# The causal mask of every first-pass unit moves from TensorE products into VectorE's row-maximum instructions

## The reference

```python
q = split_heads(x @ Wq + bq)
k = split_heads(x @ Wk + bk)
v = split_heads(x @ Wv + bv)
att = jnp.einsum('bhtd,bhsd->bhts', q, k) * (1.0 / math.sqrt(Dh))
causal = jnp.tril(jnp.ones((T, T), dtype=bool))
att = jnp.where(causal[None, None], att, -jnp.inf)
att = jax.nn.softmax(att, axis=-1)
o = jnp.einsum('bhts,bhsd->bhtd', att, v)
```

## Time and profile before

| | |
|---|---|
| median of 3 runs | 521.52 us |
| lowest and highest of them | 516.39 and 522.48 us |
| span of the profiled execution | 517.1 us |
| TensorE products busy | 468.1 us (91%), 3122 instructions |
| VectorE busy | 374.1 us (72%), 1046 instructions |
| ACT busy | 272.8 us (53%) |
| POOL busy | 252.8 us (49%) |

### The profile page before, as it was taken

The page is one execution under the profiler, slowest core; times in us unless marked ns, Lnnn a source line. Parts: engine busy times, 40 slices in busy tenths (PEclk is TensorE's granted clock), DMA queues, the critical chain, the costliest instruction groups (busy, mean ns, idle before and its releaser), DMA issues. The chain is left out here.

```text
span 517.1 us, 9099 instructions
## 1 busy us (share of the span) xinstructions
PE 468.1 (91%) x3122; PEld 239.6 (46%) x3122; DVE 374.1 (72%) x1046; ACT 272.8 (53%) x571; POOL 252.8 (49%) x344
## 2 busy tenths in 40 slices
PE   3478889999999999999999999999999998899897
PEld 2224334544644553545454453545454454344554
DVE  4687746997589748985699648985789757875165
ACT  2214554775558535765568435764567534755321
POOL 7534356533865077535764077525763251523530
PEclk9857996999999999999999999999999999999999
DMA  4674452332333234323443134323433222003000
GB/s 106 164 171 115 117 152 50 85 94 85 106 99 87 56 113 117 100 69 106 114 101 90 42 111 112 97 61 104 129 83 98 83 77 60 2 2 104 1 21 22
DMA packets 40942, 45.31 MB, mean 88 GB/s; under 512 B 9448, under 2 KB 32520, under 8 KB 40896
## 3 DMA queue, kind: packets, MB, share of 16 engines
q1 hardware_dynamic: 35652, 40.92, 29.9%
q10 hardware_dynamic: 5244, 3.82, 2.6%
HBM read 33.70 MB, written 10.61 MB: 86 GB/s over the span
## 5 line engine op out<-in xcount | busy, mean ns | idle before, releaser
L799 ACT ACTIVATE probs<-s_bank 128x512 f32<-128x512 f32 x320 | 179.9, 596 | 97.2 <-PE s_bank L1199 95.6
L979 DVE CUSTOM_DVE_ANT_0 s_bank<-s_bank,causal_row 128x512 f32<-128x512 f32 (+1 forms) x256 | 156.2, 642 | 28.9 <-PE s_bank L1179 27.3
L1179 PE MATMUL s_bank<-k_stack,q_stack 72*128 72x256 bf16 (+3 forms) x512 | 129.6, 314 | 10.7 <-DVE row_max L979 5.1
L1199 PE MATMUL s_bank<-q_stack,k_stack 75*128 75x128 bf16 (+3 forms) x512 | 120.4, 308 | 15.3 <-DMA q_stack<-max_rows 7.6
L662 POOL TENSOR_SCALAR_AFFINE_SELECT probs<-probs 128x512 f32<-128x512 f32 (+1 forms) x96 | 75.5, 794 | 116.2 <-ACT probs L799 116.0
L1199 PEld LDWEIGHTS s_bank<-q_stack,k_stack 75*128 75x128 bf16 x512 | 43.1, 100 | 92.0 <-ACT probs L799 41.1
L1218 PE MATMUL pv_bank<-probs,v_aug 128*32 128x512 f32 (+3 forms) x1024 | 83.2, 444 | 0.0
L1179 PEld LDWEIGHTS s_bank<-k_stack,q_stack 72*128 72x128 bf16 x512 | 47.3, 100 | 75.0 <-DVE row_max L979 38.5
L984 DVE TENSOR_REDUCE row_max<-s_bank 128x2 f32<-128x512 f32 (+1 forms) x96 | 64.5, 687 | 16.9 <-PE s_bank L1183 16.0
L1218 PEld LDWEIGHTS pv_bank<-probs,v_aug 128*32 128x32 f32 x1024 | 26.1, 110 | 43.8 <-issue 34.2
L1067 DVE SCALAR_TENSOR_TENSOR silu_sb<-tanh_sb,gate_bank 128x512 f32<-128x512 f32 x38 | 26.1, 687 | 21.6 <-ACT tanh_sb L852 21.3
(11 more groups left out here) (183 smaller groups left out, 546.0 us busy)
## 6 DMA issues: line engine op xcount, KB each, us to landing
k_stack<-k_scr SPq DMA_DIRECT2D x96, 96.0 KB
q_stack<-q_scr SPq DMA_DIRECT2D x93, 96.0 KB
coef_all<-coef_scr SPq DMA_DIRECT2D x28, 256.0 KB, 3.9
k_scr<-k_parts SPq DMA_DIRECT2D x32, 96.0 KB, 1.9
q_scr<-q_parts SPq DMA_DIRECT2D x31, 96.0 KB, 1.9
k_scr<-k_parts SPq DMA_DIRECT2D x32, 64.0 KB, 1.8
x_res<-in_L_attn_x SPq DMA_DIRECT2D x8, 256.0 KB, 3.7
x_in<-in_L_attn_x ACTq DMA_DIRECT2D x7, 256.0 KB, 2.8
```

The lines of the kernel that those rows point to most:

```text
L799: nc.scalar.activation(dst, src, ACT.Exp, scale=SCALE).then_inc(exp_done, 1)
L979: nc.vector.tensor_tensor_reduce(out=s1_bank[u % 2][:, 0:w], in0=s1_bank[u % 2][:, 0:w], in1=causal_row[:, T - w:T], scale=1.0, scalar=MAS ...
L1179: final = nc.tensor.matmul(dst[:, w * i:w * (i + 1)], q_stack[0:KROWS, h, P * qt:P * (qt + 1)], k_stack[0:KROWS, h, 0:w], start=(i == 0), ...
L1199: final = nc.tensor.matmul(dst[:, at:at + w], k_stack[0:MROWS, hh, P * j:P * (j + 1)], q_stack[0:MROWS, hh, P * j:T], start=True, stop=True)
```

## The change

VectorE takes the maximum of every unit with the masked instruction, once for each head of the unit; the reduction is gone. TensorE's mask products are gone, and so are `causal` and its two instructions of set-up on POOL. Units 8 and 9 become two masked maxima of 256 elements each, unit 10 four of 128 elements each, every one with its reading of the accumulator; only the last of a unit raises `s1_reduced`. The rest of the diff rewrites the way in which the program walks through the table `ORDER` (a list of turns instead of loops, and a count of the uses of a bank made from that list). The words of the table are the same, and apart from the instructions named no engine's sequence changes.

```diff
-            causal = sb("causal", [P, P], BF16)
...
-            nc.gpsimd.memset(causal[:, :], 0.0).then_inc(const_step, 1)
+            nc.gpsimd.memset(ones_wide[:, :], 1.0).then_inc(const_step, 1)
...
-            final = nc.gpsimd.affine_select(out=causal[:, :], in_=causal[:, :], compare_op=ALU.is_ge, fill=MASKED,
-                                           base=0, pattern=[[-1, P]], channel_multiplier=1)
...
-                    if masked_by_max(a):
-                        if u == 0 and it == 0:
-                            dve.wait_ge(row_masked, 1)
-                        nc.vector.tensor_tensor_reduce(
-                            out=s1_bank[u % 2][:, 0:w], in0=s1_bank[u % 2][:, 0:w], in1=causal_row[:, T - w:T], scale=1.0,
+                    if u == 0 and it == 0:
+                        dve.wait_ge(row_masked, 1)
+                    for i in range(nh):
+                        scores = s1_bank[u % 2][:, w * i:w * (i + 1)]
+                        final = nc.vector.tensor_tensor_reduce(
+                            out=scores, in0=scores, in1=causal_row[:, T - w:T], scale=1.0,
                             scalar=MASKED, op0=ALU.add, op1=ALU.max,
-                            accum_out=row_max[s % 2][:, 0, h, qt].unsqueeze(1)).then_inc(s1_reduced, 1)
-                    else:
-                        nc.vector.reduce_max(row_max[s % 2][:, 0, h:h + nh, qt],
-                                             s1_bank[u % 2][:, 0:nh * w].rearrange("p (h k) -> p h k", h=nh),
-                                             AX_X).then_inc(s1_reduced, 1)
+                            accum_out=row_max[s % 2][:, 0, h + i, qt].unsqueeze(1))
+                    final.then_inc(s1_reduced, 1)
...
-                                                 k_stack[0:KROWS, h, 0:w], start=(i == 0), stop=masked_by_max(a))
-                    if not masked_by_max(a):
-                        diagonal = dst[:, 0:nh * w].rearrange("p (h k) -> p h k", h=nh)[:, :, w - P:w]
-                        final = nc.tensor.matmul(diagonal, ident_bf[:, :], causal[:, :].unsqueeze(1).to_broadcast([P, nh, P]),
-                                                 start=False, stop=True)
+                                                 k_stack[0:KROWS, h, 0:w], start=(i == 0), stop=(i == nh - 1))
```

More of the change, by code:

```diff
@@ L80 @@
 ORDER = {
+    "head": {
+        "pe": "cond xt k q v gates",
+        "dve": "xs cond xn cols k q gates",
+        "act": "xt k q stack v gates",
+        "pool": "xs late",
+        "sp": "stack",
+    },
     "first": {
@@ L168, in task, with turn_task @@
     return (int(parts[1]), parts[0], int(parts[2]) if len(parts) > 2 else 0)
[L171 to L182, removed]
+def turn_task(it, word):
+    if word[0] == "-":
+        return (it - 1, *task(word[1:]))
+    if word[0] == "+":
+        return (it + 1, *task(word[1:]))
+    return (it, *task(word))
+TURNS = [("head", -1), ("first", 0), *(("middle", b) for b in range(1, B - 1)), ("final", B - 1), ("tail", B)]
+ENGINES = ("pe", "dve", "act", "pool", "sp")
+PROGRAM = {e: [turn_task(it, word) for plan, it in TURNS for word in ORDER[plan][e].split()] for e in ENGINES}
 FILL_TAIL = {("y", 0): 2, ("x2t", 0): 9, ("g", 0): 2}
 MISC_TASKS = ("o", "ot", "x2t", "lg", "ct", "xt", "q", "k", "v", "max")
[L190 to L196, removed]
+MISC_RANK = {x: n for n, x in enumerate(
+    x for x in PROGRAM["pe"] if x[2] in MISC_TASKS and (x[0], x[2]) not in ((-1, "k"), (-1, "v")))}
 def misc_at(it, use):
[L201 to L209, removed]
+    return MISC_RANK[(it, *use)]
 def wait_v(eng, b, misc_read, v_read):
@@ L216, in wait_v, with walk @@
     else:
-        eng.wait_ge(misc_read, misc_at(b - 1, (s_of(b - 1, "v"), "v", 0)) + 1)
-def turn_of(s, name, a):
-    return (B - 1, s, name[1:], a) if name[0] == "-" else (B, s, name, a)
+        eng.wait_ge(misc_read, misc_at(b - 1, (0, "v", 0)) + 1)
 def need(eng, sem, value):
-    if not isinstance(value, int) or value > 0:
+    if value > 0:
         eng.wait_ge(sem, value)
[L231 to L243, removed]
+def walk(engine, run):
+    for x in PROGRAM[engine]:
+        run(*x)
 def block_kernel(nc, x, Wq, bq, Wk, bk, Wv, bv, Wo, bo, gamma, beta, router, w_gate, w_up, w_down,
@@ L408, in first @@
         def first(it):
-            return isinstance(it, int) and it == -1
+            return it == -1
         def last(it):
[L412 to L417, removed]
+            return it == B
         def gate_of(it, a):
@@ L533, in run @@
                 if name == "cw":
-                    sp.wait_ge(misc_read, misc_at(it, (s_of(it, "ct"), "ct", 0)) + 1)
+                    sp.wait_ge(misc_read, misc_at(it, (0, "ct", 0)) + 1)
                     for landed in coef_landed:
@@ L555, in has_next @@
             def has_next(it):
-                return not isinstance(it, int) or it < B - 1
-            walk(sp, "sp", run)
+                return it < B - 1
+            walk("sp", run)
             sp.wait_ge(stored, 16 * (B + 1))
@@ L703, in run @@
                     nc.gpsimd.tensor_tensor(cp[2], coef_rest[:, :, :], cp[1], ALU.subtract).then_inc(coef_split, 1)
-            walk(pool, "pool", run)
+            walk("pool", run)
         @block.scalar
@@ L852, in run @@
                     nc.scalar.activation(tanh_sb[:, :], gate_of(it, a)[:, :], ACT.Tanh, scale=0.5).then_inc(tanh_ready, 1)
-            walk(act, "act", run)
+            walk("act", run)
         @block.vector
@@ L1090, in run @@
                                                 (x_in if last(it) else x2)[:, tiles, :], ALU.add).then_inc(out_half if last(it) else gate_read, 1)
-            walk(dve, "dve", run)
+            walk("dve", run)
         @block.tensor
@@ L1141, in run @@
                     nc.tensor.matmul(gate_bank[:, 0:C], bv_rep[:, :], wo[:, :], start=True, stop=True).then_inc(bias_mm, 1)
-                if name == "v" and isinstance(it, int) and it == 0:
+                if name == "v" and it == 0:
                     pe.wait_ge(ffn_in, 16 * FFN_DMAS)
@@ L1286, in run @@
                     if a == 0:
-                        pe.wait_ge(misc_read, misc_at(it, (s_of(it, "x2t"), "x2t", 0)) + 1)
+                        pe.wait_ge(misc_read, misc_at(it, (0, "x2t", 0)) + 1)
                     if a == 0 and it == 1:
@@ L1314, in run @@
                     if a == 0:
[L1315 removed]
+                        pe.wait_ge(misc_read, misc_at(it, (0, "ct", 0)) + 1)
                         pe.wait_ge(x2_ready, it)
@@ L1341, in run @@
                         last_mm.then_inc(down_written, 1)
-            walk(pe, "pe", run)
+            walk("pe", run)
 _INS = ["L0_attn_x", "L0_attn_Wq", "L0_attn_bq", "L0_attn_Wk", "L0_attn_bk", "L0_attn_Wv", "L0_attn_bv",
```

8 lines of the change are left out of this document (3 added, 5 removed).

## The result

The changed kernel takes 548.81 us as the median of 4 runs (544.2 to 549.62), the kernel before 519.7 us (516.39 to 522.48) beside it: a ratio of 1.0549, with a 95% interval of 1.0469 to 1.0629. (A ratio leaves out the runs that took over 1.5% more than the fastest of their kernel; in experiments e1 and e4 those are the ones with the lowest granted clock, so there it understates the loss that the median shows.) The prediction was 526.8, in a range of 516 to 540; the time lies above it. The profiled execution has a span of 547.9 us, 30.8 more than before.

A forecast was written before the change was run, and what follows sets the result against it. No single bound: TensorE and VectorE wait for each other in turn. Six middle batches at +0.89 us give +5.3, first and last 0; 521.5 + 5.3 = 526.8 us, range 516 to 540.

The forecast's parts named there:

- The step from the two pair lengths that the trace showed to the two that it didn't: VectorE's maximum-and-reading pairs: a straight line from 512 and 384 elements gave 0.38 us for 256, 0.25 for 128.
- The sum at a steady clock: Delays at the ends of the four groups of a middle batch: 0.60 + 0.06 + 0.23 = 0.89 us.
- Group 2: Its end: later bank release moves TensorE's waiting product by 0.76 us, partly absorbed before the maxima's transposition; +0.60 us.
- Groups 0 and 1: Their ends: removed mask time turns into waiting; 0 for group 0, +0.06 us for group 1.
- Group 3: Its end: unit 10's four pairs release later, so POOL's split and the maxima's transposition come late; +0.23 us.
- the last rival: TensorE's granted clock falls once more per middle batch, 1.62 us each, giving 536.5 us; chance 0.14.
- TensorE as the bound: Rival: the mask products' 14.1 us come off whole, giving 507.4 us; chance 0.05.
- VectorE as the bound: Rival: all 22 us of VectorE's added time appear, giving 543.5 us; chance 0.09.
- A floor in the pair: Rival: no VectorE pair takes under 0.51 us, losing 38 us in all, giving 559.5 us; chance 0.05.
- The period of 61.6 us: Middle batch: about 57.9 us was forecast; near 60 or more would show that VectorE's time was on the path.
- the granted clock below 1.00: Sign against the forecast: TensorE's granted clock below 1.00 in most middle stretches.
- VectorE's busy time: Sign for the forecast: it rises by some 50 to 65 us, more than 22 because the rows overlap.

The follow-up runs named there:

- e1: Changed kernel with units 8 to 10 of group 2 back to mask product and reduction in every batch; 527.11 us, ratio 1.0067.
- e4: Kernel before without its 96 mask products, reductions kept and nothing put in their place; 533.49 us, ratio 1.0179.
- e7: Kernel before with the second layer norm's statistics moved behind unit 10 of group 2 on VectorE; 545.82 us, ratio 1.0542.
- e2: Kernel before with only units 8 to 10 of group 2 masked by VectorE as in the change; 547.34 us, ratio 1.0546.
- e5: Changed kernel with five products that nothing reads in TensorE's two waits at the end of group 2, each middle batch; 528.53 us, ratio 1.0225.
- e3: Changed kernel with a product of zeros on TensorE where each mask product stood; 552.74 us, ratio 1.0616.

## Why the prediction was wrong

**What held.** The step from the two pair lengths that the trace showed to the two that it didn't (0.38 and 0.25 us) was right to 0.01. The Trainium skill, "VectorE: DVE Perf Modes", section on the TRN2 errata, would give 0.39 and 0.26 as an estimate; the trace lies 0.01 below each. The sum at a steady clock was nearly right too: +0.66 us measured for a middle batch, +0.89 forecast. By its terms:

- *Group 2*, +0.60 forecast: +0.67. Counted from unit 8, TensorE's product that waits for the bank comes 0.69 us later than before, less than the 0.76 of the sum, and nothing absorbs any of it on the way to the transposition of the maxima, where 0.16 had been allowed for. The two errors cancel.
- *Groups 0 and 1*, +0.06: the table's first four lines give -0.01 - 0.22 + 0.15 + 0.04 = -0.04.
- *Group 3*, +0.23: -0.22 + 0.25 = +0.03. The masked unit takes 1.09 us to its release (193.97 to 195.06), 1.14 forecast; and before, the transposition came 0.71 us after POOL's split had begun (180.76, 181.47), now 0.56 (195.15, 195.71): TensorE's own work had held it up by 0.15.

**What failed** is the step that left TensorE's clock out of the sum: the forecast has no term for it, and the last rival, which has one, was wrong in both of its numbers, price and chance. The price, 1.62 us for a fall, was read from one fall of 3.4 us in the kernel before (284 to 287). The trace of before had another, at 75.4 to 85.6 us, three times as long: there group 0, up to the start of group 1, took 14.70 us, and the same stretch of e7 and e2, whose clock stays up there, takes 10.99 and 11.08, so that this fall cost 3.6 to 3.7. The falls of the changed kernel are of that kind and cost 3.97. Six of them are 24 us, the lateness 6 x 0.66 = 4. The other 3 are about 4 in the first batch, where the prediction had 0 with 1 us either way and where the clock is low from 19 to 56 us and again from 63 to 66 (before: 21 to 38 and 41 to 48), and 1 in the second, less the 1.6 of the fall at 284 that the kernel before had. The rival as written, with the other price, would have said 521.5 + 5.3 + 24 = 551.

Its chance was 0.14 because "the longest wait, at 167.92, is moved and not lengthened". That was the wrong wait to look at. The fall comes before that wait, after two shorter ones at the first products of group 3, 0.27 us and none before, 0.61 and 0.31 after. The prediction had worked out the 0.76 us by which these come later, and used it for the path alone. It never asked what TensorE does in that time, although the 0.44 us of removed products, in the same place, make the idle time longer still: it went from 0.44 to 1.27 us. That is the step that failed. The delay was nearly right; that it costs only itself was not. It cost 0.66 us a batch on the path and 3.97 by the clock; e5 shows that without the idle time the same delay is followed by no fall there, and e4 that falls come without any delay.

**The other rivals.** TensorE as the bound: at a steady clock the products were worth 0.77 us a batch, less than half of their own time, so the case against it was right; with the clock as it came, taking them out alone cost time (e4). VectorE as the bound at 543.5 us came near the time by accident: e2 has a quarter of its added instructions and all of the loss. A floor in the pair isn't there.

**The signs that were named.** The period of 61.6 us stood in the list as a sign of VectorE's time, and the granted clock below 1.00 as a sign of its own. Both came; only the second was the cause. A period that is too long must be read with the clock's row beside it. VectorE's busy time rose by 20 us and not by 50 to 65, because the page's line for the engine counts overlapping instructions once; added up over the page's groups (239.3 + 73.2 us after, 156.2 + 64.5 + 36.2 before) it rose by 55.6.

## What to carry to other kernels

Where TensorE runs at its upper level with little idle time to spare, cost a change by what it does to TensorE's *standing still*, place by place, and price a fall by the longest one that the trace shows. Here 0.7 us of added waiting cost 0.7 us on the path and 4 us by the clock, and taking products away without any delay cost more time than it saved. Products that nothing reads, put into waits that are there anyway, gave 6.4 us back to the kernel before and 20 to the changed one.

## What was not expected of the hardware

VectorE's four normalising instructions took 1.11 to 1.12 us in a middle batch of the changed kernel and of the kernel before, 0.28 each, and 2.56 us in the two kernels with the statistics moved, 0.64 each. In the rows of e7 above, POOL's three `AFFINE_SELECT` instructions ran through nearly all of it (292.06 to 294.35). In the last batch they take 2.66 us in the kernel before too, and there too POOL is busy for most of it (447.61 to 449.75, of 447.67 to 450.33). The Trainium skill, "SBUF — State Buffer", section "Who interferes with whom", tells that such an instruction of VectorE can take a pair of ports that it shares with GpSimd, and that the later of the two then waits; these rows would agree, but no run here was made to show it. And equal stretches of TensorE end in a fall or not (the batches of e3), so the times of one kernel spread with its clock: in e1 518.62 us at a mean of 0.957, and 530.99 at 0.929.
